# A decoder layer on one core: key blocks written by eight masked copies, context projected a group ahead, second buffers in the last group

## The reference

```python
x = x + gla(layernorm(x))              # convolution of 4 taps, silu, q k v g, gated linear
                                       # attention with 8 heads, norm by head, gate, wout
x = x + xattn(layernorm(x), ctx)       # 16 heads of 8; softmax(q k / sqrt(8)) v, then Wo
x = x + ffn(layernorm(x))              # the best 48 of 64 positions by a router's score are
                                       # replaced by gelu(x @ w_block), the others pass

q = (Q @ Wq.T).reshape(B, S, H, Dk).transpose(0, 2, 1, 3)
k = (K @ Wk.T).reshape(B, S, H, Dk).transpose(0, 2, 1, 3)
v = (V @ Wv.T).reshape(B, S, H, Dk).transpose(0, 2, 1, 3)
attn = softmax(einsum('bhqd,bhkd->bhqk', q, k) / sqrt(Dk))
ctx = einsum('bhqk,bhkd->bhqd', attn, v)
```

## Time and profile before

| | us |
|---|---|
| median of 3 runs | 375.64 (374.22 to 376.35) |
| profiled execution | 373.81 |
| its span, first to last instruction | 372.1 |
| busy: PE, DVE, ACT, POOL | 281.2, 244.3, 202.6, 178.2 |

### The profile page before, as it was taken

How to read it: one execution, slowest core, us unless ns; L and a number is a source line. 1 busy time by engine, 2 the same in 40 slices (tenths; PEclk the granted TensorE clock), 3 DMA queues, 4 the chain that set the end, 5 groups by cost and what they waited for, 6 DMA issues and landing times.

```text
span 372.1 us, 9366 instructions
## 1 busy us (share of the span) xinstructions
PE 281.2 (76%) x3570; PEld 199.0 (53%) x3570; DVE 244.3 (66%) x534; ACT 202.6 (54%) x342; POOL 178.2 (48%) x216
## 2 busy tenths in 40 slices
PE   0123572778989898989898989898988989869730
PEld 0002561564676567656755775677657746635520
DVE  3740554537788689868986898679866666626223
ACT  5051254236845882698459745974595367436201
POOL 8446523642395168617852775156517512241143
PEclk9999896889999999999999999999999999999755
DMA  3700301010110102010401031101020300000000
GB/s 74 216 0 10 89 11 24 13 32 16 48 34 8 25 15 65 4 26 13 120 7 25 13 85 43 23 13 33 13 49 15 87 17 16 28 4 2 28 0 28
DMA packets 17596, 12.73 MB, mean 34 GB/s; under 512 B 3856, under 2 KB 14608, under 8 KB 17552
## 3 DMA queue, kind: packets, MB, share of 16 engines
q1 hardware_dynamic: 17552, 12.14, 13.2%
HBM read 4.79 MB, written 2.10 MB: 19 GB/s over the span
## 4 chain that ended last, share of the span: by engine, by line
PE 39%; ACT 19%; issue 13%; DVE 10%; SPq 8%; POOL 4%; DMA 1%; POOLq 0%; ACTq 0%; DVEq 0%
PE AT L679 8%; SPq L237 5%; PE S L747 5%; ACT pr L1073 5%; PE PA L696 4%; PE PT L771 4%; ACT prT L1078 4%; DVE y L1256 3%; SPq L246 3%; PE AT L618 2%; ACT L1042 2%; PE S L757 2%; PE PB L733 2%; DVE at L1302 2%; PE PB L784 2%
## 5 line engine op out<-in xcount | busy, mean ns | idle before, releaser
L1354 DVE TENSOR_REDUCE nmax<-S 128x16 bf16<-128x1024 f32 x32 | 39.1, 1222 | 37.8 <-PE S L747 37.8
L1078 ACT COPY prT<-PT 128x512 f32<-128x512 f32 x64 | 37.0, 579 | 19.9 <-PE PT L771 19.7
L771 PE MATMUL PT<-ident,pr 128*128 128x128 f32 x256 | 40.6, 281 | 8.5 <-ACT prT L1078 7.0
L458 POOL TENSOR_TENSOR kc<-ke,e_r 128x512 f32<-128x512 f32 x32 | 39.9, 1276 | 11.3 <-issue 11.3
L679 PE MATMUL AT<-q_bd,kc 128*64 128x128 f32 x512 | 34.5, 291 | 14.2 <-DVE at L1302 5.6
L784 PEld LDWEIGHTS PB<-v_x,prT 128*64 128x64 f32 x1024 | 34.9, 137 | 16.2 <-issue 12.1
L784 PE MATMUL PB<-v_x,prT 128*64 128x18 f32 x1024 | 40.9, 213 | 1.1 <-ACT prT L1078 0.3
L679 PEld LDWEIGHTS AT<-q_bd,kc 128*64 128x64 f32 x512 | 30.9, 147 | 17.4 <-issue 12.5
L771 PEld LDWEIGHTS PT<-ident,pr 128*128 128x128 f32 x256 | 27.7, 141 | 23.3 <-issue 10.9
L1073 ACT ACTIVATE pr<-S,rs 128x1024 f32<-128x1024 f32 x32 | 35.7, 1117 | 7.3 <-PE S L757 7.3
L747 PE MATMUL S<-k_bd,qT 64*64 64x512 f32 x256 | 34.8, 614 | 4.8 <-ACT pr L1073 4.0
(11 more groups left out here) (146 smaller groups left out, 659.7 us busy)
## 6 DMA issues: line engine op xcount, KB each, us to landing
q_bd<-qs SPq DMA_DIRECT2D x128, 8.0 KB
cT<-in_ctxT SPq DMA_DIRECT2D x8, 256.0 KB, 3.2
v_bd<-vt SPq DMA_DIRECT2D x32, 64.0 KB, 2.1
k_bd<-kx SPq DMA_DIRECT2D x128, 16.0 KB
out<-yout SPq DMA_DIRECT2D x8, 256.0 KB, 2.5
x_all<-in_x SPq DMA_DIRECT2D x1, 256.0 KB, 2.8
wv_s<-in_wv SPq DMA_DIRECT2D x1, 64.0 KB, 2.1
wg_s<-in_wg SPq DMA_DIRECT2D x1, 64.0 KB, 2.0
```

Of the source, the lines that this page charges most:

```text
L458: nc.gpsimd.tensor_tensor(kc[:, i * NCH * L:(i + 1) * NCH * L].rearrange("p (c d s) -> p c d s", c=NCH, d=NCH), kev[:, i, :, :].unsqueeze( ...
L771: last = nc.tensor.transpose(PT[:, P * p:P * p + P], pr_v[:, i % 2, P * (hp * n + p):P * (hp * n + p) + P], ident[:, :])
L1078: nc.scalar.copy(prT[:, 512 * n:512 * n + 512], PT[:, :]).then_inc(s_prT, 1)
L1354: nc.vector.tensor_reduce(nmax[:, :], cut(S, XH, L), AX.X, ALU.max, negate=True).then_inc(s_max, 1)
```

## The change

The key blocks are no longer spread by DMA. `a_keys` now has four parts of two instructions each: an ACT copy of the whole projected tile from PSUM into one of eight slots of `k_bd`, with a scale by row that is one in the rows of two heads (h and h + 8) and zero elsewhere. `keys_to_blocks`, `kx`, `clear_keys` and 128 DMAs go. The context of group a = n + 2 is projected in step n, keys and values side by side in the two banks of S between the last exp of the step and the first `x_scores` of the next, and `v_x` has two buffers. The first `x_scores` of a step waits for all copies of the group after its own.

In the last group, which has no stage a beside it, the tiles alternate between S and AT, PT and PA0, PB and PA1. `nmax` and `rden` have two halves. DVE takes over centring, `own`, `tiedb`, `cnt` and the result for group 7. The loads are reordered (first x, conv, a-weights, Wk and Wv, context 0, x of group 1, context 1, the rest), the queries of groups 0 and 1 are spread by eight DMAs of SP and eight of ACT, `q_bd` is cleared in four parts, and the written-out orders of all five engines are changed.

```diff
+    SHARED = 2
+    QP = 4
+    KPARTS = 4
-        kx = sb("kx", GT)
+        k_rows = sb("k_rows", XHG)
-        v_x = sb("v_x", SEQ * PAIRS * 2 * VC)
+        v_x = sb("v_x", 2 * SEQ * PAIRS * 2 * VC)
+        def s_buf(g, i):
+            return AT if g == NG - 1 and i % 2 else S
+        def pt_buf(g, n):
+            return PA0 if g == NG - 1 and n else PT
+        def pv_buf(g, i):
+            return PA1 if g == NG - 1 and i % 2 else PB
...
@@ SP
-                for n in range(NB):
+                for n in range(0, NB, 2 if g < SHARED else 1):
-            def keys_to_blocks(g):
...
             sp.dma_start(xa[:, 0:TPG, :], x_tiles[:, 0:TPG, :]).then_inc(x_in, 16)
+            sp.dma_start(conv_s[:, :], conv_w).then_inc(w_conv, 16)
             load(WEIGHTS, w_in)
-            sp.dma_start(xa[:, TPG:NT, :], x_tiles[:, TPG:NT, :]).then_inc(x_rest, 16)
+            load(KEYS, w_keys)
+            load_ctx(0)
+            sp.dma_start(xa[:, TPG:2 * TPG, :], x_tiles[:, TPG:2 * TPG, :]).then_inc(x_next, 16)
+            load_ctx(1)
             load(LATER, w_later)
+            sp.dma_start(xa[:, 2 * TPG:NT, :], x_tiles[:, 2 * TPG:NT, :]).then_inc(x_rest, 16)
@@ POOL
-            def clear_queries(g):
-                nc.gpsimd.memset(q_bd[:, :], 0.0).then_inc(q_clear, 1)
-            def clear_keys(g):
-                nc.gpsimd.memset(k_bd[:, :], 0.0).then_inc(k_clear, 1)
+            def clear_queries(g, part):
+                cols = NB * KH // QP
+                nc.gpsimd.memset(q_bd[:, cols * part:cols * part + cols], 0.0).then_inc(q_clear, 1)
@@ PE
             def context_keys(g):
-                pe.wait_ge(s_at, 2 * (g + 1))
-                nc.tensor.matmul(AT1, WkT_s[:, :], cT[:, GT * (g % 2):GT * (g % 2) + GT], start=True, stop=True).then_inc(s_KX, 1)
+                pe.wait_ge(s_kx, KPARTS * g)
+                if g > 1:
+                    pe.wait_ge(s_exp, TPG * (g - 1))
+                nc.tensor.matmul(S[:, 0:GT], WkT_s[:, :], cT[:, GT * (g % 2):GT * (g % 2) + GT],
+                                 start=True, stop=True).then_inc(s_KX, 1)
             def x_scores(g, i):
                 if i == 0:
                     pe.wait_ge(s_qT, g + 1)
-                    pe.wait_ge(s_kbd, 16 * XH * (g + 1))
-                    pe.wait_ge(s_vx, g + 1)
+                    pe.wait_ge(s_kx, KPARTS * upto(g + 2))
+                    pe.wait_ge(s_vx, upto(g + 2))
+                elif g < NG - 1:
+                    pe.wait_ge(s_exp, TPG * g + i)
+                elif i == 1:
+                    pe.wait_ge(s_at, 2 * NG)
                 else:
-                    pe.wait_ge(s_exp, TPG * g + i)
+                    pe.wait_ge(s_exp, TPG * g + i - 1)
@@ ACT
-            def a_keys(g):
+            def a_keys(g, part):
                 act.wait_ge(s_KX, g + 1)
-                act.wait_ge(s_kbd, 16 * XH * g)
-                nc.scalar.copy(kx[:, :], AT1).then_inc(s_kx, 1)
+                if g > 1:
+                    act.wait_ge(s_S, TPG * (g - 1))
+                for h in range(2 * part, 2 * part + 2):
+                    last = nc.scalar.activation(k_bdv[:, g % 2, h, :], S[:, 0:GT], ACT.Copy, scale=k_rows[:, h:h + 1])
+                last.then_inc(s_kx, 1)
+            def queries_to_blocks(g):
+                for n in range(1, NB, 2):
+                    nc.scalar.dma_start(q_bdv[8 * n:8 * n + 8, n, :], qs[8 * n:8 * n + 8, :]).then_inc(s_qbd, 16)
@@ DVE, last group
+            def last_norm(g):
+                for i in range(TPG):
+                    last = nc.vector.tensor_scalar(xn3[:, E * i:E * i + E], x2[:, E * i:E * i + E],
+                                                   mv3[:, 2 * i:2 * i + 1], rs3[:, i:i + 1], ALU.subtract, ALU.mult)
+            def last_result(g):
+                nc.vector.tensor_tensor(yout[:, :], xn3[:, :], x2[:, :], ALU.add).then_inc(s_yout, 1)
@@ PE, end of step(n)
-                context_values(b)
+                gla_out(b)
                 x_out(n)
                 if has(a):
-                    scores(a, 0)
+                    context_values(a)
                 x_out2(n)
...
```

More of the change, by code:

```diff
@@ L546, in step @@
                     route(c)
+                if has(a + 2):
+                    scale_a(a + 2)
                 group_norm(b)
+                if has(a):
+                    spans(a)
                 if has(c):
@@ L959, in a_features @@
                 act.wait_ge(s_conv, TAPS * g)
-                nc.scalar.copy(xpad_v[:, :, TAPS - 1:PADL], cut(PA0, SEQ, L)).then_inc(s_xpad, 1)
+                nc.scalar.copy(xpad_v[:, :, TAPS - 1:PADL], cut(PT if g == 1 else PA0, SEQ, L)).then_inc(s_xpad, 1)
             def a_silu(g):
@@ L1072, in b_exp @@
                 col = TPG * (g % 2) + i
-                nc.scalar.activation(pr_v[:, i % 2, :], S[:, :], ACT.Exp, scale=rs2[:, col:col + 1]).then_inc(s_exp, 1)
+                if g == NG - 1 and i > 1:
+                    act.wait_ge(s_PT, 2 * (TPG * g + i - 1))
+                nc.scalar.activation(pr_v[:, i % 2, :], s_buf(g, i)[:, :], ACT.Exp, scale=rs2[:, col:col + 1]).then_inc(s_exp, 1)
             def b_probs(g, i, n):
```

595 lines of the change are left out of this document (331 added, 264 removed).

## The result

The changed kernel takes 359.75 us (median of four, 358.1 to 364.7) against 375.49 us before (374.2 to 376.4); the ratio is 0.957 with an interval of 0.952 to 0.962, so it is 4.3% faster. Forecast were 349 us and a range of 337 to 361. (A few executions of these kernels are slower as a whole, with a lower granted clock; the medians include them and the ratios do not, so a median can stand a little above what its ratio says.)

The account below looks back on a forecast made before the run. PE was taken to bound the seven steps, chains of waits the prologue and tail. Prologue -13.0, steps -9.8, last group -4.0 and tail -0.2 sum to -27.0: 373.81 becomes 346.8, with the median's offset 348.6, said as 349; range 337 to 361.

Parts of the forecast that it names:

- the steps do not shorten: Rival: seven steps stay about 36 us, PE's saving at the seam returning as waits for ACT mid-step; 358 us, chance 0.17.
- The steps: Seven middle steps: each falls from 36.1 to 34.7 us, PE waiting less at the seam; -9.8 us.
- the walk: One step, PE and ACT followed in turn: small new waits mid-step, 1.5 us in sum, giving 34.7 us.
- The prologue: Up to the first `x_scores`: memset dropped, issues split and group 1 earlier, from 81.95 to 69 us; -13.0.
- the issuing is the price: Prologue: SP's 10.86 us of issuing 16 `qs` copies, split over two queues, brings `scores` of group 0 4.8 us earlier.
- ScalarE gives the memset's gain back: Prologue: ACT's added copies and gate cost 4.3 us against 4.1 gained, so `qs` of group 0 stays at 28.3 to 28.4.
- The last group: Last group's cross attention: with S and AT, scores run beside max and exp, 22.8 to 18.8 us; -4.0.
- The tail: After the last division: DVE's faster normalisation (-1.0) and result (-0.6) against later ranks (+1.4); -0.2, between -1.5 and +1.

Follow-up runs that it names:

- both chains freed: Changed kernel with half the query issues for groups 2 to 7 and new orders on GpSimd, TensorE and VectorE: 357.26 us, ratio 0.955.
- less TensorE work: Changed kernel with half of the attend products, values' projection and context's values left out from group 2 on: 353.21 us, ratio 0.940.
- both: Changed kernel with the cuts of "less TensorE work" plus the half query issues and orders of "both chains freed": 355.15 us, ratio 0.948.

## Why the prediction was right on the whole and wrong in the steps

The range held, but by 1.3 us, and the time is that of the rival "the steps do not shorten" (358) rather than the forecast's 349. Three terms of the sum had their mechanism right; the largest error, 12.6 us, is in the fourth.

**The steps, -9.8 predicted, +2.8 measured: the step that failed.** The prediction cut 1.4 us from each step by walking TensorE and ScalarE once through it and adding 1.5 us of small waits to TensorE's 33.2. Measured in the middle step are 2.7 us of idle time and 33.84 of work. Of the idle time 0.7 us is for ScalarE (0.3, 0.2 and 0.2), less than the walk had. But 1.7 us is for the two engines that it left out: 0.91 for GpSimd's `norm_b3`, and 0.46 and 0.34 for VectorE's mask and last division. ScalarE's copies were also added up as if they did not overlap: 4.9 us a step were forecast, and its busy time rose by 3.9 (24.16 to 28.05).

Two things make up the 12.6 us. First, 1.6 us of the sum is the clock. The last step ran at 0.95 (31.33 us). In profiles where the clock stayed at 1.00 it took 29.77, and 34.34 where it fell to the lower level of 1.2 GHz for a while. Three windows show it, the last step of the run with half the queries, that of the run with both chains freed, and the ten us of the latter at the lower clock:

```profile
282.61:312.38 29.77, 24.24 (x308) 15.69 (x307) 19.51 (x46) 16.57 (x24) 6.86 (x8) 1.00 0.04 11
```
```profile
281.50:315.84 34.34, 28.50 (x311) 19.33 (x311) 19.77 (x46) 16.46 (x24) 7.27 (x9) 0.85 0.03 10
303.70:314.00 10.30, 8.74 (x60) 7.57 (x60) 3.93 (x16) 1.94 (x4) 2.12 (x3) 0.50 0.09 26
```

Second, the steps from the second to the sixth did not shorten, and no single wait explains it. The timeline of one middle step, cut at ScalarE's four `exp` (L1073 before, L1098 after), shows where each change goes:

| kernel | `x_scores` to exp 0 | to exp 1 | to exp 2 | to exp 3 | to next `x_scores` | step |
|---|---|---|---|---|---|---|
| before | 3.14 | 5.59 | 5.77 | 6.23 | 15.41 | 36.14 |
| after | 3.67 | 5.16 | 6.51 | 4.91 | 16.27 | 36.52 |
| both chains freed | 3.73 | 6.38 | 6.51 | 4.90 | 14.70 | 36.22 |
| less TensorE work | 3.14 | 4.96 | 6.52 | 4.91 | 15.79 | 35.32 |
| both | 3.28 | 6.14 | 6.51 | 4.90 | 14.71 | 35.54 |

The seam, the last stretch, did not get shorter but longer by 0.9. The mask's wait shrank by 0.6 and three attends (1.5 us) left it, but the context's key projection (1.0) and the transposes of x2 (0.6) came in, with the wait of 0.91 for `norm_b3`. Moving the transposes away again (both chains freed) shortened it by 1.6 and lengthened the stretch that received them by 1.2, of which 0.66 is the transposes and 0.64 the new wait for `nmax`. The middle, up to exp 3, fell by 0.5 as a whole (20.73 to 20.25), and not by more: from exp 1 to exp 2 the time is 6.50 to 6.52, in all steps but the last, in all thirteen profiles of the changed kernel and its variants. It is so too where half of the values' projection, 0.45 us of TensorE's work in this very stretch, is left out; a wait for `prT` of 0.18 and a longer one of 0.35 take its place. (Exp 2 to exp 3 is as steady, 4.9 us, but there no run changed TensorE's work, and ScalarE waits 0.28 for it.) The trace shows no gap of ScalarE from exp 1 to exp 2, and the change has moved `ab` and `ex`, 0.87 us, into it; it was 5.77 before:

```profile
150.61 1.12 ACT L1098 ACTIVATE pr<-S,rs 128x1024 f32<-128x1024 f32 x1
151.62 0.42 ACT L1017 ACTIVATE ab<-qk 128x256 f32<-128x256 f32 x1
152.07 0.42 ACT L1019 ACTIVATE ex<-ab 128x256 f32<-128x256 f32 x1
152.50 1.28 ACT L1064 ACT_TABLE_LOAD   x1
...
154.91 1.28 ACT L1069 ACT_TABLE_LOAD   x1
...
157.12 1.11 ACT L1098 ACTIVATE pr<-S,rs 128x1024 f32<-128x1024 f32 x1
```

TensorE's idle time in this step went from 2.9 (36.14 - 33.23) to 2.7 us, and its busy time from 33.23 to 33.84 with the same matmuls. Several groups of them took 5% longer, as the transposes of `on` (272 ns before) and `wq` (379 before) do here; why is open.

```profile
L583 PE MATMUL PA<-ident,on 128*128 128x128 f32 x4 | 0.7, 287 | 0.0
L636 PE MATMUL PA<-xcT,wq_s 128*64 128x256 f32 x4 | 0.7, 404 | 0.0
```

So the rival "the steps do not shorten" came true in its number and not in its mechanism: it had the seam save and ScalarE's middle spend, and it was the seam that took in as much as it gave. The sign that the prediction named for it, steps of 36 with many waits for `prT`, came by half: these waits fell from 0.9 to 0.3 us.

Shown by runs: no one of `norm_b3`, the key copies, the query issues or the key products sets the step, nor all but the copies together; and of 1.4 us of TensorE's work cut, 0.7 reach the step. Argued from the trace and from the one cut in that stretch: that ScalarE from exp 1 to exp 2 is the firmest of the limits. Two runs that would test the rest were not made: one with `ab` and `ex` ahead of exp 1 again, and one with fewer key copies on top of both cuts, where `xT` waits behind six of them. So what sets 36 us stays open in part.

**The prologue, -13.0 predicted, -11.0 measured: right.** That the issuing is the price is shown by the run on one queue (3.7 us at the first `scores`, 8.5 at the first `x_scores`). It was priced 1 us too high at the first `scores`: a gain of 4.8 forecast, 3.8 measured. The rule of the Trainium skill ("DMA: Bandwidth & Descriptors", Issuing engines are not separate DMA queues) that issuing is usually small beside the transfer does not hold for 16 copies of this size: 10.9 us of issues, 3.7 us lost at the first `scores` alone. The forecast that ScalarE gives the memset's gain back was right too (`qs` 28.73, forecast 28.3), and the run with the memset put a number on it: 1.1 of 3.3 us survive. The missing 2 us stand at `qs` of group 1 already (55.85, forecast 53.4), and they are mostly the clock: the second half of `scores` of group 0 took 3.68 us. In seven of the other nine profiles with this prologue it took 1.97, and there `qs` of group 1 is at 52.8 to 53.9. (The first half of `scores` of group 1 at the lower clock is no part of the miss, since the forecast counted it so.) In the ten profiles 67.9 is the middle of the first `x_scores`, on the other side of the forecast 69.

**The last group, -4.0 predicted, -3.5 measured: right**, with 19.3 us for the forecast 18.8. Taking the banks and their orders away makes it 24.4.

**The tail, -0.2 predicted, -2.1 measured: mis-sized, and outside its own bounds of -1.5 and +1.** The chain was as described. 1.4 us of the surprise is the transposes and the output projection at the upper clock, a term that the sum did not have. From the transposes of x2 to the end the forecast had +0.8 (+1.4 and -0.6) and measured is +0.2 (13.81 against 13.61): the router behind the ffn costs 0.8 us, where the ranks were to start 2 us later.

The four errors, +2.0, +12.6, +0.5 and -1.9, make 13.2 us, which is what the profiled execution was missed by (359.99 against 346.8). The time was missed by only 10.8, because the forecast added 1.8 us from profiled execution to median and 0.4 by rounding, and the median came out 0.2 below the profiled execution; that part is luck.

## What to carry to other kernels

Here one engine was busy for 93% of a pipelined step with a fixed order, and each wait removed turned up elsewhere. In such a step forecast a gain at a fraction of the wait (here 0 to 0.3 us of 0.9), walk all engines through it and not only the two fullest, and first ask which stretch of the helper engines has no gap. Cutting the step at a recurring operation of the second engine, as in the table above, shows in one look where moved work lands. What paid here was in the parts that are chains (prologue, last group): the issues of many small copies split over two queues, and banks of their own for independent tiles.
